# Expert 0's first tile without the tables, zero fills on GpSimd's queue, final gathers behind the needed stores alone

## What is computed

```
x = x + xcond(layernorm(x), ctx_2048, ctx_2048, itok)     # per sequence: 8 heads of 16 channels, 512 positions
x = x + ffn(layernorm(x), gate_w, w1, w2, w3)
# ffn, for each of 16*128 = 2048 tokens:
probs = softmax(xt @ gate_w.T); weights, indices = top_k(probs, 2); weights /= weights.sum()
x1 = silu(xt @ w1[e].T); x3 = xt @ w3[e].T; expert_out[e] = (x1 * x3) @ w2[e].T
out = sum over the two chosen experts of weight * expert_out
```

## Time and profile before

| what | value |
|---|---|
| three runs | 1257.71, 1259.67, 1263.73 us; median 1259.67 |
| profiled execution | 1256.96 us, span 1255.3 us |
| TensorE busy | 1073.0 us (85%) |
| VectorE busy | 811.7 us (65%) |
| GpSimd busy | 607.2 us (48%) |
| ScalarE busy | 409.5 us (33%) |
| DMA | 189.57 MB, mean 151 GB/s |

### The profile page before, as it was taken

How to read it: one execution, slowest core, us unless ns; L and a number is a source line. 1 busy time by engine, 2 the same in 40 slices (tenths; PEclk the granted TensorE clock), 3 DMA queues, 4 the chain that set the end, 5 groups by cost and what they waited for, 6 DMA issues and landing times.

```text
span 1255.3 us, 19968 instructions
## 1 busy us (share of the span) xinstructions
PE 1073.0 (85%) x5113; PEld 420.3 (33%) x5114; DVE 811.7 (65%) x964; ACT 409.5 (33%) x734; POOL 607.2 (48%) x547
## 2 busy tenths in 40 slices
PE   1799999999999999851999999998999999999900
PEld 0223333333333333210444444443444444444400
DVE  5977777777777877213743965938577495953445
ACT  3266666666666666721111111111101101110100
POOL 6444666666666661222810843807466283820045
PEclk9999999999999999975999999999999999999955
DMA  6454555555555543005654755747566475743368
GB/s 181 137 180 130 162 163 163 162 162 162 162 162 162 162 130 80 35 22 184 193 101 96 222 134 164 186 100 222 129 194 174 142 201 165 186 117 85 75 190 263
DMA packets 210793, 189.57 MB, mean 151 GB/s; under 512 B 137248, under 2 KB 176160, under 8 KB 205344
## 3 DMA queue, kind: packets, MB, share of 16 engines
q1 hardware_dynamic: 197280, 120.91, 37.2%
q0 software_dynamic: 12896, 67.12, 16.4%
q10 hardware_dynamic: 576, 1.05, 0.2%
HBM read 107.50 MB, written 50.86 MB: 126 GB/s over the span
## 4 chain that ended last, share of the span: by engine, by line
PE 64%; POOL 8%; DMA 8%; DVE 7%; issue 7%; ACT 4%; SPq 1%; POOLq 0%; DVEq 0%; ACTq 0%; PEldq 0%
PE rows L1078 25%; PE heads_out L1078 13%; PE heads_out L989 7%; PE rows L962 6%; PE scores L976 6%; POOL W L433 4%; ACT W L592 4%; DVE nm L715 3%; DMA W<-parts_dram 3%; PE misc L1038 2%; POOL W L432 2%; PE misc L1059 1%; POOL U L556 1%; PE misc L1015 1%; DMA U<-U 1%
## 5 line engine op out<-in xcount | busy, mean ns | idle before, releaser
L1078 PE MATMUL rows<-W,U 128*128 x1776 | 391.6, 381 | 26.1 <-DMA U<-stage 22.8
L715 DVE TENSOR_REDUCE nm<-rows 128x2 f32<-128x1024 f32 x256 | 305.4, 1220 | 58.9 <-PE rows L962 48.4
L592 ACT ACTIVATE W<-scores 128x512 f32<-128x512 f32 x512 | 282.9, 598 | 161.8 <-PE scores L976 156.7
L1078 PEld LDWEIGHTS rows<-W,U 128*128 128x128 bf16 x1776 | 174.2, 98 | 238.4 <-issue 32.2
L661 ACT ACTIVATE U<-rows 128x512 f32<-128x512 f32 x78 | 46.4, 597 | 518.0 <-PE rows L1078 509.0
L1078 PE MATMUL heads_out<-W,U 128*128 x888 | 199.5, 381 | 14.0 <-issue 11.1
L962 PE MATMUL rows<-W,U 96*128 96x512 bf16 x512 | 163.7, 404 | 48.6 <-DMA W<-parts_dram 27.8
L976 PE MATMUL scores<-U,W 128*128 128x512 bf16 x512 | 179.6, 386 | 14.0 <-ACT W L592 4.9
L433 POOL TENSOR_TENSOR W<-U,W 128x2048 bf16<-128x2048 f32 x42 | 172.4, 4104 | 7.7 <-POOL W L432 7.7
L900 DVE TENSOR_TENSOR U<-rows,U 128x512 f32<-128x512 f32 x78 | 53.6, 688 | 182.5 <-ACT U L661 182.2
L907 DVE TENSOR_TENSOR U<-U 128x512 bf16<-128x512 f32 x78 | 161.1, 2065 | 2.7
(11 more groups left out here) (142 smaller groups left out, 677.9 us busy)
## 6 DMA issues: line engine op xcount, KB each, us to landing
U<-wpack_dram POOLq DMA_DIRECT2D x42, 1024.0 KB, 5.8
parts_dram<-U SPq DMA_DIRECT2D x32, 384.0 KB, 4.1
U<-parts_dram SPq DMA_DIRECT2D x32, 384.0 KB, 4.2
W<-parts_dram SPq DMA_DIRECT2D x32, 384.0 KB, 5.2
stage<-slots_dram SPq DMA_DIRECT2D x39, 256.0 KB, 3.0
expert_out_dram<-U SPq DMA_DIRECT2D x39, 256.0 KB, 3.1
parts_dram<-U SPq DMA_DIRECT2D x32, 256.0 KB, 4.0
stage<-wpack_dram POOLq DMA_DIRECT2D x12, 512.0 KB
```

The costliest lines, as they stand in the source:

```text
L592: s.activation(probs[:, w % 2, j, kk, :], sc[u % 2][:, :], ACT.Exp) \
L715: v.tensor_reduce(nm[:, bb.parity, 2 * k:2 * k + 2], p1[k % 2][:, :].rearrange("p (c k) -> p c k", c=2), AX_X, ALU.max, negate=True).then_ ...
L1078: ins = m.matmul(bank, part_of(s_part, k), W[:, bass.ds(at_w, 512)], start=(k == 0 and n == 0), stop=(k == n_chunks - 1 and n == 2))
```

## The change

Tile 0 always is the first 128 rows of `zs`, so SyncE loads it by a fixed address once the scatters have landed, and TensorE starts `up_tile(0)` with fixed operands, before it waits for `tab_ready`. For this, rows 0 to 127 are zeroed early (in slot 0, from a zeroed `z` buffer), and expert 0's own zero fill begins at row 128 or later. In the same place GpSimd writes zeros to the seven tiles of `ys` that may not be needed. The eight zero fills behind the slots all go to GpSimd's queue. SyncE waits for them after the load of tile 0 and ahead of the load of tile 1. GpSimd loads expert 1's weights once the turned rows of tiles 0 and 1 have landed (`xt_in`) and no longer at the landing of tile 0's rows. The gathers wait for the stores of needed tiles alone, by two counts from a new row of `etab`.

```diff
-            sp.wait_ge(S["cv_zero"], 1)
-            sp.wait_ge(S["zero_ready"], 1)
-            for e in range(0, E, 2):
-                r = sp.value_load(etab[0:1, 0, e:e + 1], min_val=0, max_val=E * REG - P)
-                sp.dma_start(zs[bass.ds(r, P), :], cv[:, :]).then_inc(S["zero_out"], 16)
-            sp.wait_ge(S["zero_out"], 16 * E)
             for i in range(2):
                 sp.wait_ge(slots_out[i], 32 * (B // 2))
-            sp.wait_ge(S["tab_ready"], 1)
...
-            for t in range(2):
-                load_row(t, t)
+            sp.dma_start(xrow[:, 0, :], zs[0:P, :]).then_inc(xrow_in[0], 16)
+            sp.wait_ge(S["zero_out"], 16 * (1 + T - SURE + E))
+            sp.wait_ge(S["tab_ready"], 1)
+            load_row(1, 1)
             for t in range(2):
                 turn_x(t, t, first=True)
                 load_row(t + 2, t)
...
+                if b.within(0, 0):
+                    g.memset(z[:, 0, :], 0.0).then_inc(S["rows_zero"], 1)
+                    hold(S["rows_zero"], 1)
+                    pool.dma_start(zs[0:P, :], z[:, 0, :]).then_inc(S["zero_out"], 16)
+                    for t in range(SURE, T):
+                        pool.dma_start(ys[t * P:(t + 1) * P, :], z[:, 0, :]).then_inc(S["zero_out"], 16)
                 pv = b.plus(-1)
...
+                    if pv.within(0, 0):
+                        hold(S["zero_out"], 16 * (1 + T - SURE))
...
+            hold(S["cv_zero"], 1)
+            hold(S["zero_ready"], 1)
+            for e in range(E):
+                r = pool.value_load(etab[0:1, 0, e:e + 1], min_val=0, max_val=E * REG - P)
+                pool.dma_start(zs[bass.ds(r, P), :], cv[:, :]).then_inc(S["zero_out"], 16)
             hold(S["attn_done"], 1)
             hold(S["tables_done"], 1)
-            hold(xrow_in[0], 16)
+            for par in range(2):
+                hold(xt_in[par], 16)
             expert(1, 1)
...
-            hold(y_out[0], 16 * ((T + 1) // 2))
-            hold(y_out[1], 16 * (T // 2))
+            for par in range(2):
+                stored = pool.value_load(etab[0:1, 2, par:par + 1], min_val=16, max_val=16 * ((T + 1) // 2))
+                hold(y_out[par], stored)
...
-            act.wait_ge(S["cv_zero"], 1)
-            act.wait_ge(S["zero_ready"], 1)
-            for e in range(1, E, 2):
-                r = act.value_load(etab[0:1, 0, e:e + 1], min_val=0, max_val=E * REG - P)
-                act.dma_start(zs[bass.ds(r, P), :], cv[:, :]).then_inc(S["zero_out"], 16)
...
-            link(v.tensor_copy(etab[:, 0, :], zero_rows))
+            link(v.tensor_copy(etab[:, 0, 1:E], zero_rows[:, 1:E]))
+            link(v.tensor_scalar(etab[:, 0, 0:1], zero_rows[:, 0:1], float(P), None, ALU.max))
...
+            link(v.tensor_scalar(count_t, tio[:, 0, 1:T + 1], cum[:, E - 1:E], None, ALU.is_le))
+            for par in range(2):
+                link(v.tensor_reduce(counts2[:, par:par + 1], count_t[:, par:T:2], AX_X, ALU.add))
+            link(v.tensor_scalar(etab[:, 2, 0:2], counts2, 16.0, None, ALU.mult))
             v.nop().then_inc(S["tables_done"], 1)
...
-            pe.wait_ge(S["tab_ready"], 1)
-            m.nop().then_inc(S["tiles_done"], 1)
...
             def up_tile(t, par, first=False):
-                ready = pe.value_load(tab[0:1, 2, bass.ds(t, 1)], min_val=1, max_val=E)
-                off = half_of(t)
-                pe.wait_ge(S["w_ready"], ready)
+                if first:
+                    off = 0
+                    pe.wait_ge(S["w_ready"], 1)
+                else:
+                    ready = pe.value_load(tab[0:1, 2, bass.ds(t, 1)], min_val=1, max_val=E)
+                    off = half_of(t)
+                    pe.wait_ge(S["w_ready"], ready)
...
             up_tile(0, 0, first=True)
+            pe.wait_ge(S["tab_ready"], 1)
+            m.nop().then_inc(S["tiles_done"], 1)
```

More of the change, by code:

```diff
@@ L160, in build @@
         tab = sb("tab", [P, 4, T + 1], I32)
-        etab = sb("etab", [P, 2, E], I32)
+        etab = sb("etab", [P, 3, E], I32)
         fidx = sb("fidx", [P, B, 2], I32)
@@ L171, in build @@
         at_base = small[:, 256:256 + 2 * B]
+        count_t, counts2 = small[:, 320:320 + T], small[:, 384:386]
         hb = U[:, 0:1024].bitcast(BF16).rearrange("p (n s i) -> p n s i", n=2, s=2)
@@ L200, in build @@
             chunk2_steps w_ready tab_ready zero_out tiles_done x_hi x_lo up_ready silu_done h_ready
-            h_hi h_lo yb_ready pool_held dve_held sp_held gexp_ready comb_steps comb_done out_done
+            h_hi h_lo yb_ready pool_held dve_held sp_held gexp_ready comb_steps comb_done out_done rows_zero
             attn_done routed cnt_ready zero_ready tables_done cv_zero table_prep""".split()
```

## The result

The changed kernel took 1244.53 us (median of 4 runs, 1244.34 to 1246.12) against 1259.37 for the kernel before: ratio 0.9883, 95% interval 0.9861 to 0.9905. It is faster by 1.2%, twice the 6.8 us that I had forecast, and outside my range of 1249 to 1255. The profiled execution took 1244.34 us with a span of 1242.8, which is 12.5 less than the span before.

What follows compares the result with a forecast made beforehand. TensorE was taken as the bound in attention and tiles, so gains lay at the tile stage's two ends. 6.4 (end) + 1.4 (first gap) - 1.0 (attention) = 6.8 off 1258.7 gave 1251.9 us, range 1249 to 1255.

Steps and rivals of the forecast that it cites:

- the 6.8 us that I had forecast: Whole kernel: gains of 6.4 at the end and 1.4 in the first gap, less 1.0 in attention.
- The end, 6.4: End of the tile stage: gathers no longer wait for dead tiles' stores, gain 6.4 us, bounds 4.5 and 7.0.
- The 0.6 that I took off: At the end: taken off the 7.0 us earlier first gather, as dead tiles' transposes share DMA engines with gathers.
- The fills in front of tile 0's transpose: Gap before the tiles: the transpose still waits for the last fill, now in one queue at a 1.3 us pitch.
- the fast queue (0.75): Rival for the fills: pitch 0.75 us, the gap gives 5.4, total gain 10.8, time 1247.9; chance 0.15.
- the slow one (2.3 and more): Rival for the single fill queue: beyond a pitch of 2.3 us the kernel is slower; chance 0.10, shared with another stall.
- The first gap, 1.4: Between attention and tiles: fills land 7.0 us later, but tile 0's transpose takes 3.2, not 7.83; gain 1.4.
- Attention, a loss of 1.0: Slot 0: early zeros compete with the reload TensorE needs; loss 1.0 us, bounds 0 and 4.3.
- the 4.3 of its rival: Rival in attention: all zeros go ahead of the reload, stall 4.3 us, total gain 3.5, time 1255.2; chance 0.12.
- The tile stage, set to zero: Tiles behind the first matmul: TensorE is the bound, the change takes no work from it; no term in the sum.
- they are hidden: Expert 1's weights, starting about 12 us later: covered by expert 0's five tiles of 15.5 us each.
- The sum against the median: Whole kernel: the 6.8 gain taken from 1258.7, the middle of all four executions, giving 1251.9.

Runs made afterwards that it cites:

- e1: Kernel before plus slot 0's early zeros, with gathers waiting for needed stores alone: 1251.22 us, ratio 0.9929 to the kernel before.
- e3: Kernel before plus only the eight early zero DMAs of slot 0: 1258.47 us, ratio 0.9978 to the kernel before.
- e6: Changed kernel with the eight fills back on SyncE and ScalarE, four each: 1244.34 us, ratio 0.9873 to the kernel before.
- k1_again: k1 unchanged, run again beside the changed kernel on one chip: 1239.82 us, ratio 0.9841 to the kernel before.
- a_after: Changed kernel, unchanged, run for a second profile: 1242.39 us, ratio 0.9869 to the kernel before.
- e2: Kernel before with expert 1's weights waiting for the turned rows of tiles 0 and 1: 1252.39 us, ratio 0.9948.
- k0: e2 with expert 1's weights also held behind the first h (h_ready 1): 1249.26 us, ratio 0.9923 to the kernel before.
- g1: Changed kernel with expert 1's weights held behind the first h (h_ready 1): 1244.17 us, ratio 0.9886 to the kernel before.
- f1: e5 with fills of even experts on GpSimd and of odd ones on ScalarE: 1244.44 us, ratio 0.9873 to the kernel before.
- k1: f1 with expert 1's weights held behind the first h (h_ready 1): 1239.18 us, ratio 0.9852 to the kernel before.
- c_before: Kernel before, unchanged, run for a second profile: 1258.03 us, ratio 0.9996.
- e4: Changed kernel with expert 1's weights again behind the landing of tile 0's rows: 1250.28 us, ratio 0.9929 to the kernel before.
- e5: Changed kernel with tile 0's transpose ahead of SyncE's wait for the fills: 1245.32 us, ratio 0.9871 to the kernel before.
- a_after_again: Changed kernel, unchanged, run again beside k1_again on one chip: 1247.03 us, ratio 0.9893 to the kernel before.

## Why the prediction was wrong, by its steps

- **The end, 6.4.** Right in its main term: the first gather moved by 7.0 behind the last product. The 0.6 that I took off is near to the 0.7 of the two profiles by luck. VectorE was free in time and waited for the gathers themselves, which landed later, and the stretch behind the first gather is 50.5 to 52.4 in traces with late gathers and 50.8 to 52.6 with early ones, so no loss is shown. The end gave 6.3 in the profile, 6.7 at the mean of all traces, 6.2 by the ratios of `e1` and `e3`.
- **The fills in front of tile 0's transpose.** Right in mechanism: the transpose went out behind the last fill's landing, and the pitch was 1.33 for the 1.3 of my sum. Neither the fast queue (0.75) nor the slow one (2.3 and more) came true.
- **The first gap, 1.4: mis-sized, 3.3 from attention's end.** The first fill started at 574.75 and not 576.0, since its value was read while GpSimd was still at its scatter. The last landed in 2.28 and not 3.28, which was a row of fills that went out on two queues at once; where they do so again, the last takes 3.27 (`e6`) and 4.24 (`k1_again`). The anatomy section of the page "DMA: Bandwidth & Descriptors" of the Trainium skill has 2.0 us plus the bytes' time, 2.6 by my estimate; the trace with one queue, 2.28, is nearer to it than to 3.28. The transpose itself took 3.46 for 3.2.
- **Attention, a loss of 1.0.** It was 0.2 in the profile and not a loss at all by `e3`. The 0.2 itself says little, as attention ended anywhere between 568.91 and 577.58 in these traces. TensorE did wait 1.0 (at 88.15) in that stretch for the reload that met the moved weight loads, but `a_after` has no such wait. The store of the row maxima landed in 1.39 us where it took 3.15 before, which I had set at nothing; `e2`, with no early zeros, has 1.40, so this is not shown to be the change. That the completion count waits for all earlier writes of its DMA engine (Trainium skill, "DMA: Bandwidth & Descriptors", queues, rings and completion order) did not make the 4.3 of its rival; no run here shows the rule itself.
- **The tile stage, set to zero: the step that failed.** I said of expert 1's weights only that they are hidden, and costed of the contention only tile 0's transpose of x; that the tiles behind the first matmul keep their length had no reason in my sum. In the profiles they gave 0.8 at down product 0 and 2.3 later. Against the forecast of 6.8 the profiled executions differ by 12.6, and of the missing 5.8 the tile stage is 3.1, the gap 1.9 and attention 0.8. Another 2.2 come from the medians: the kernel before was 2.4 slower at its median than in the execution that I had profiled, the changed one 0.2 (1244.53 and 1244.34). Over more traces the tile stage is shorter by some 5 us (598.7 to 603.9 against 595.1 to 597.0), and the medians leave about as much for it: 14.8 - 3.3 for the gap - 6.7 for the end = 4.8.
- **What the runs showed in its place.** For down product 0: the time of those loads alone moves it by 1.7 us (`e2` to `k0`), 2.1 (after to `g1`) and 4.2 (`f1` to `k1`, two traces), and the traces have two ways for it, VectorE's split beside GpSimd's passes and the turn of h beside the loads. A wait of TensorE there can have a low clock behind it, which costs up to 2.9 more (`c_before`, seen at down product 1). Moving the loads behind the transposes gives 6.5 us in all (`e2`), of which the gap explains 4.6. Its opposite, weights ahead of the transpose, costs the changed kernel 4.5 to 7.5 us by the ratios of different chips (`e4`), and in its trace only the gap is longer, by 3.6.
- **What stays open.** The cause of the 2.3 is not shown. At down product 16, far from any edit, both profiles of the kernel before lose 3.7 to 3.8 us, `e2` 3.9, and all others between 1.5 and 2.0. In the two of the kernel before the low clock then adds 1.7. The three traces of the changed kernel never had it, nor had `e1`, `e3` and `k0`, which keep the fills and tile 0 as before (`e1` has one like it at down product 12). Near it too, turns of h and weight loads leave together (at 873.70 and 873.72 in the profile before), but which edit keeps it away, or whether chance does, was not settled; nor why `e3` is 0.2% faster.
- **The sum against the median.** Taking the mid of four executions, 1258.7, was fair for the kernel before (medians of 1257.8 to 1260.4 in all later runs). The spread in it, 6 us between the three executions that I had and 7 to 10 in four of five later sets (2 in the fifth, of seven executions), was a sign that I read as noise. In the changed kernel it is 1.8 to 2.5 us on each chip, in sets of only four to six.

## What to carry to other kernels

- A load that is hidden has a price where it starts: 2 MB that nobody waits for put off the first matmul by 4.6 us because they were issued a microsecond ahead of the transpose that everybody waited for, and holding them back gave 6.5 in all. Ask of each prefetch not only whether it is in time, but what is on the critical path in its first ten microseconds, and hold it behind that.
- If executions of a kernel differ by 6 us or more, profile it more than once before a forecast: the stalls that come and go are where the gain may be. Then compare stretches over several traces, and say of each trace where its execution stands among the times.
- A shortcut in the data's path brings nothing as long as the queue that serves it still has the old wait in front. Moving `turn_x(0)` ahead of the fill wait brought the first matmul 4.4 earlier, and only with the weights held back further (`k1` against `f1`) did the median follow.

## What the runs showed of the hardware that I had not expected

- A fill of 256 KB with an address from a value load goes out of GpSimd's queue every 1.33 us, though the DMA occupies the engine for only 0.54; a run of seven without such a load took 3.76 us, 0.54 apart:

```profile
65.41 0.79 POOL L496 DMA_DIRECT2D slots_dram<-z  x1 [0.72 <-POOL z L494]
66.20 3.76 POOL L498 DMA_DIRECT2D expert_out_dram<-z  x7
```

- The DMA transpose of tile 0's x took 3.15 to 3.5 us with no weight load near, 3.91 with zero fills still going out (`e5`), 7.83 to 7.94 with two loads of 1 MB issued 0.9 us ahead of it (four traces), and 6.75 with them 3.0 us ahead (`e4`).
- VectorE's split of a half of h took 0.43 and 0.69 us alone. Beside GpSimd's passes over 2048 columns its two operations took up to 4.27 (`k0`, at 646.00) and 4.49 (the changed kernel, at 691.43).
- After waits of 2.25 to 3.6 us at a down product the next 24 matmuls took 7.0 us and not 5.35 in `before`, `c_before` and `e1` (7.04, 7.01, 7.00), with a granted clock of 0.55, 0.51 and 0.53 in their first 3.5 to 3.8 us; after 3.75 us in `e2` they took 5.35 at a clock of 1.00.
- The end of attention moved by up to 8.1 us (`g1` 569.49, `k1_again` 577.58) in kernels with the same code there, and by 5.9 on one chip (`a_after_again` 571.64, `k1_again` 577.58).
